# GpSimd's series of sums, bias additions and weight splits moved behind VectorE's low parts and normalised tokens

## The reference, cut to what matters

```
x = x + xattn(layernorm(x), ctx)     # self attention, add+LN1, cross attention, add+LN2,
                                     # relu(x@w1+b1)@w2+b2 (512 -> 2048 -> 512), add+LN3 (gain g3, bias be3)
x = x + ffn(layernorm(x))            # gates of 8 experts, top 2; all experts share w1, w2:
                                     # relu(x@w1)@w2, scaled by the sum of the two gate weights
```

## Time and profile before

| | |
|---|---|
| median of 3 runs | 519.07 us (518.35 to 520.5) |
| profiled execution, its own time | 519.52 us |
| its span, first to last instruction | 517.7 us |
| TensorE matmul busy | 507.8 us, 98% |
| VectorE busy | 364.7 us, 70% |
| ScalarE busy | 236.5 us, 46% |
| GpSimd busy | 136.5 us, 26% |
| mean granted TensorE clock | 1.000 |

### The profile page before, as it was taken

The page is one execution under the profiler, slowest core; times in us unless marked ns, Lnnn a source line. Parts: engine busy times, 40 slices in busy tenths (PEclk is TensorE's granted clock), DMA queues, the critical chain, the costliest instruction groups (busy, mean ns, idle before and its releaser), DMA issues.

```text
span 517.7 us, 7623 instructions
## 1 busy us (share of the span) xinstructions
PE 507.8 (98%) x2970; PEld 486.7 (94%) x2970; DVE 364.7 (70%) x633; ACT 236.5 (46%) x416; POOL 136.5 (26%) x102
## 2 busy tenths in 40 slices
PE   7999999999999999999999999999999999999997
PEld 6899999889988888989999999999999899999996
DVE  3843769796799985886499776378594387596645
ACT  3853652475688975254644333206615534152210
POOL 2530540104032135055404000805541440210000
PEclk9999999999999999999999999999999999999999
DMA  8941212031689861224421232002220022202004
GB/s 243 346 177 58 64 77 81 1 116 57 230 285 332 304 217 35 81 75 97 98 77 68 93 151 82 1 1 82 81 82 1 1 82 81 82 0 82 2 0 128
DMA packets 18444, 53.76 MB, mean 104 GB/s; under 512 B 1640, under 2 KB 2440, under 8 KB 15848
## 3 DMA queue, kind: packets, MB, share of 16 engines
q1 hardware_dynamic: 18348, 53.20, 31.1%
q10 hardware_dynamic: 60, 0.07, 0.1%
HBM read 51.63 MB, written 1.64 MB: 103 GB/s over the span
## 4 chain that ended last, share of the span: by engine, by line
PE 89%; DVE 4%; DMA 3%; ACT 2%; issue 1%; SPq 0%; POOL 0%; DVEq 0%; ACTq 0%
PE ps L736 18%; PE ps L738 18%; PE ps L737 18%; PE ps L782 4%; PE ps L781 4%; PE ps L780 4%; PE ps L836 2%; PE ps L810 2%; PE ps L978 2%; PE ps L980 2%; PE ps L979 2%; DMA tok<-x_in 2%; PE ps L952 2%; PE ps L954 2%; PE ps L953 2%; DMA cnR<-ctxn_in 1%
## 5 line engine op out<-in xcount | busy, mean ns | idle before, releaser
L736 PE MATMUL ps<-AH,WH 128*128 128x400 f32 x284 | 98.9, 348 | 1.3 <-DVE AL L1496 1.1
L738 PE MATMUL ps<-AH,WL 128*128 128x400 f32 x284 | 98.0, 345 | 0.0
L737 PE MATMUL ps<-AL,WH 128*128 128x400 f32 x284 | 97.9, 345 | 0.0
L736 PE MATMUL ps<-XH,WH 128*128 128x400 f32 x224 | 78.0, 348 | 0.1
L738 PE MATMUL ps<-XH,WL 128*128 128x400 f32 x224 | 77.3, 345 | 0.0
L737 PE MATMUL ps<-XL,WH 128*128 128x400 f32 x224 | 77.2, 345 | 0.0
L601 POOL TENSOR_TENSOR WL<-WR,WH 128x512 fp32r<-128x512 f32 x34 | 48.4, 1452 | 73.9 <-ACT WH L1142 73.9
L736 PEld LDWEIGHTS ps<-AH,WH 128*128 128x128 f32 x284 | 53.3, 188 | 3.0 <-DVE AL L1496 2.6
L737 PEld LDWEIGHTS ps<-AL,WH 128*128 128x128 f32 x284 | 53.4, 188 | 0.0
L738 PEld LDWEIGHTS ps<-AH,WL 128*128 128x128 f32 x284 | 53.4, 188 | 0.0
L1142 ACT ACTIVATE WH<-WR 128x512 fp32r<-128x512 f32 x64 | 36.3, 624 | 20.6 <-DMA WR<-wts_in 20.6
(11 more groups left out here) (243 smaller groups left out, 1134.3 us busy)
## 6 DMA issues: line engine op xcount, KB each, us to landing
WR<-wts_in SPq DMA_DIRECT2D x19, 1024.0 KB, 4.8
ctR<-ctxt_in SPq DMA_DIRECT2D x16, 722.0 KB, 5.9
cnR<-ctxn_in SPq DMA_DIRECT2D x16, 512.0 KB, 5.2
cnR<-ctxn_in SPq DMA_DIRECT2D x8, 256.0 KB
tok<-x_in SPq DMA_DIRECT2D x4, 384.0 KB, 10.1
tok<-x_in SPq DMA_DIRECT2D x1, 1536.0 KB
cnR<-ctxn_in SPq DMA_DIRECT2D x8, 160.0 KB
VR<-wvo_in SPq DMA_DIRECT2D x4, 256.0 KB, 6.8
```

What stands on the lines that cost most here:

```text
L736: pe.matmul(dst, wh, half(mh, h, k), start=(k == 0), stop=False)
L737: pe.matmul(dst, wh, half(ml, h, k), start=False, stop=False)
L738: mm = pe.matmul(dst, wl, half(mh, h, k), start=False, stop=(k == KC - 1))
```

## The change

GpSimd gets two new waits, and one of its waits and one of its steps are changed. The four block sums of U_F+2 wait for VectorE's low part of group 3 of (U_F,0). The eight additions of be3 to tok wait for VectorE's low part of group 3 of (U_F+6,0), where they waited for TensorE's group 1 of it. `inverse_deviation(7, 0)` is moved ahead of the low parts of U_M, and these now wait until all four tiles of `normalise(3,0)` are written. Nothing is added to or removed from the work itself.

```diff
             split_weights(U_F + 1)
             inverse_deviation(5, 1)
+            pool.wait_ge(dve_evac, dve_count(U_F, 0, KC - 1))
             sum_blocks(U_F + 2)
             sum_features(0)
             sum_blocks(U_F + 4)
             pool.wait_ge(xres_loaded, 32)
             pool.wait_ge(gb_loaded, 32)
-            pool.wait_ge(gemm_done, gemm_count(U_F + 6, 0, 1))
+            pool.wait_ge(dve_evac, dve_count(U_F + 6, 0, KC - 1))
             for b in range(B):
                 pool.tensor_tensor(tok[:, b, :], tok[:, b, :], be3b[0:T, :], ALU.add).then_inc(xres_ready, 1)
             inverse_deviation(6, 0)
+            inverse_deviation(7, 0)
+            pool.wait_ge(tok_ready, 8 * 3 + HB)
             split_weights(U_M)
-            inverse_deviation(7, 0)
             split_weights(U_M + 1)
             split_weights(U_M + 2)
             inverse_deviation(8, 1)
```

## The result

The changed kernel takes 525.90 us (median of 6; 525.09 to 527.53) against 519.23 us before (6 runs on the same chips; 518.35 to 520.5): the ratio is 1.013, 95% interval 1.0111 to 1.0149, so it is 6.7 us slower. The profiled execution took 525.65 us with a span of 523.8 us. TensorE is busy for 97% and its mean granted clock is 0.993, where it was 1.000.

The account below looks back on a forecast made before the run. It took TensorE, busy 98% of the span, as the bound: stalls of 5.7 and 1.7 us, less 0.6 gained, plus 0.2 for latencies, gave +7.0 on 519.5, so 526.5 us; range 523.5 to 529.5.

Parts of the forecast that it names:

- early gain: TensorE's waits for VectorE's AL at 235.78 and 330.22 shrink by 0.37 and 0.22 us, together 0.6.
- Steps 1 to 4, the first stall: Late low parts of U_M delay the next load and ScalarE's XH; TensorE stalls 5.7 us ahead of (U_M,0).
- Steps 5 and 6, the second stall: The second load comes late too; TensorE waits 1.7 us for AL of group 3 in (U_M+1,0).
- The clock is the open cost ... and so I take zero: TensorE's granted clock stays 1.00 through the stall, cost zero; other end, half speed until (U_M,0) ends, 10.5 us more.
- rival A: Clock falls in the 5.7 us stall, (U_M,0)'s group 0 and transposes 3.8 us longer, no second stall: 528.6; chance 0.25.
- The gap is there at a lower clock: Listed sign of being wrong: TensorE's gap ahead of (U_M,0) appears, but with a lower clock.
- The sum: Whole kernel: +5.7 + 1.7 - 0.6 = +6.8, with 0.2 for the new hops' latencies +7.0, so 526.5 us.
- 525 to 528: Forecast case's own range in us: later tok_ready adds 0.9, slowed splits 0.4, XH let through sooner at most 2.2 off.
- the only term that takes something off: If ScalarE's and VectorE's order lets XH through sooner than the row distances say, at most 2.2 us less.
- the range: Whole kernel between 523.5 and 529.5 us.

Follow-up runs that it names:

- e1: Changed kernel with the third edit undone, so only the block sums' and be3 additions' new waits remain: 518.61 us against 518.87 for the kernel before.
- e4: Changed kernel with ScalarE's high parts of U_M+1 and U_M+2 moved behind groups 0 and 3 of (U_M,0), all waits kept: 524.91 us against 518.97 before.
- e7: Changed kernel, but only the last of U_M's four low parts waits for the tokens, the first three standing ahead of inverse_deviation(7,0): 522.13 us against 519.09 before.
- e6: Changed kernel with 48 extra TensorE transposes of the identity between (U_M-1,1) and (U_M,0), inside the stall: 526.72 us, ratio 1.014 to the kernel before.
- e5: As e4, with inverse_deviation(8,1) also moved ahead of U_M+2's low parts in GpSimd's order: 518.38 us against 518.97 for the kernel before.
- e3: Changed kernel without the token wait, inverse_deviation(7,0) staying ahead of U_M's low parts: 524.14 us, ratio 1.0097 to the kernel before.
- e8: Changed kernel, but the first two of U_M's low parts stand ahead of the token wait, behind inverse_deviation(7,0): 524.58 us, ratio 1.0106 to the kernel before.
- e2: Kernel before with the third edit alone, inverse_deviation(7,0) ahead of U_M's low parts and these behind the token wait: 526.57 us, ratio 1.0148.

## Why the prediction was right

It said 526.5 and +7.0; measured are 525.9 and +6.7. One of its steps failed all the same, the one on the clock. Step by step:

- **The early gain** was 0.6: measured in the traces 0.34 us at the first wait and 0.21 at the second, by e1 0.3 us of time with an interval from 0 to 1.1. A third gap shrank as well, at 358.24 of the kernel before (at 357.07 after), from 0.44 to 0.29 us; e1 still has it, so that is the third edit's.
- **Steps 1 to 4, the first stall**: 5.7 us forecast, 5.68 measured. Each hop kept its distance: load readable 4.85 us behind the low parts (4.87), XH 1.57 us behind it, XL 0.52. Here the prediction was right for its reasons: e4 shows that ScalarE's order carries the stall, e7 that the end of the low parts sets its size.
- **Steps 5 and 6, the second stall**: 1.7 us forecast, none in the changed kernel. The mechanism exists: it shows in e6 (1.8 us) and e7 (1.27 us). It was hidden by what I had set to zero. In the changed kernel AL of group 3 ends 385.50 - 371.36 = 14.1 us behind TensorE's restart, 13.9 forecast; but TensorE wants it 385.77 - 371.36 = 14.4 us behind, where 12.2 was forecast.
- **"The clock is the open cost ... and so I take zero" is the step that failed.** It fell to 0.50 in the stall. Group 0 took 1.96 us more and the transposes behind it 0.32: 2.3 us, not the 3.8 of rival A, which had the right mechanism and kept the low clock too long. "The gap is there at a lower clock" was also the text's own sign of being wrong, and it showed. The Trainium skill, "TensorE: Matmul & The Clock Gate", Part 1, was the better guide than the nearest row; by its rule the clock falls in an idle stretch, and the trace after agrees, with 1.2 GHz from near 369.3 until 376.
- **The sum** came out because the two replace each other: 5.7 + 2.3 - 0.7 = +7.3 with the clock, 5.7 + 1.7 - 0.6 + 0.2 = +7.0 without. The trace has 397.28 - 391.21 = 6.1 us behind the stalls (the transposes of half 1), and 1.0 us more for this execution's lead at 210 us: 7.1. e6 shows that this isn't chance alone: once TensorE is late by itself, the wait for AL in (U_M+1,0) has passed. That the two are nearly of one size, 2.3 and 1.8 us, is luck; with the low clock for as long as in rival A, the sum would have been 1.5 us higher. The 0.45 us between the profiled execution and the median, which I left in, are of the size of what remains. The narrow range of "525 to 528" has an upper end that its terms give (526.5 + 0.9 + 0.4) and a lower end that they don't: the only term that takes something off, 2.2 us, gives 524.3.

So the range and the sign rest on the first stall, which was understood; the last 2 us of the number were right by a substitution that the text listed under a rival.

## What to carry to other kernels

When a wait is added to an engine off the critical path, follow what is queued behind its last output, not only who uses that output: here the weights themselves were ready 1.9 us early (363.75, where TensorE was through with its earlier work at 365.68), and the cost came through the one raw buffer, the load behind it and an in-order engine that stood at the load with TensorE's next operand in its queue. A late producer can be made free by moving such a queued operand ahead of the wait for the load, but every queue on the way has to be cleared; with one cleared, the stall moved 20 us on (e4), with both it was gone (e5). And a stall's price can include a slow clock behind it, which can stand in for a second stall, so that removing one of the two may gain nothing (e6).

## What the runs showed of the hardware that was not expected

- **GpSimd's series can hold VectorE longer than one instruction.** A VectorE instruction with two SBUF inputs stood behind four GpSimd instructions for 4.69 us (e3) and behind two for 2.26 us (e8), and GpSimd's own ran at 1.23 to 1.25 us each, undisturbed (one trace each). The Trainium skill, "SBUF — State Buffer", section "SBUF: two separate sides", says that whichever of the two starts first has the shared ports for the whole instruction. The kernel before agrees with it: beside eight be3 additions in a row, the low parts took 0.74 to 1.38 us and not the 11 us of the series, and the additions took 11.02 us instead of 10.03; beside three weight splits the low part took 1.36 us (the rows under e8). So neither the operation nor the series as such decides who comes next. What does is open; no run here separates it.
- **The gap's length doesn't tell by itself whether the clock falls.** It fell in gaps of 5.68, 5.59, 4.77 and 4.40 us (changed kernel, e2, e4, e3), stayed at 1.00 through one of 1.87 us (e7) and one of 1.52 us (e8), fell behind one of 1.97 us (e8: 0.84 in the window from 358 to 360, 0.50 from 360 to 362), and fell behind two of 0.54 and 1.27 us (e6), while e7's and e8's later gaps of 1.27 us left it alone.
